# A selective-scan block on one core: the second sequence's input term scaled on ScalarE, ScalarE's longer stages cut into parts, one more slot for the broadcast rows

## The chip, the cores and the metric

The kernel runs on one core of one Trainium2 chip. The metric is the device time of one execution in microseconds; lower is better. Engines are named as the profile names them: PE is TensorE (PEld its weight loads), DVE is VectorE, ACT is ScalarE, POOL is GpSimd, SP is SyncE, which here only issues DMAs; ACTq is the DMA queue that ACT issues into.

## The reference

Two sequences of 1024 tokens with 512 channels (all float32) go through a selective scan and a feed-forward layer, each followed by a residual and a layer norm. Cut to what matters here:

```python
xn = x * rsqrt(mean(x*x) + 1e-6) * norm_w
xn = xn * sigmoid((xn @ select_proj_w.T + select_proj_b) * select_gate)
delta, B, C = split(xn @ x_proj_w.T)
delta = softplus(delta @ dt_proj_w.T + dt_proj_b)
def step(h, dt, b, c, xt):
    h = exp(dt[:, :, None] * A) * h + (dt * xt)[:, :, None] * b[:, None, :]
    return h, einsum('bdn,bn->bd', h, c)
x = layernorm(x + (y + x * D_param) @ out_proj_w.T)
x = layernorm(x + ffn(x))
```

The state h has 2 x 512 x 128 numbers, and each of the 1024 steps needs the state of the step before.

## The kernel before, in words

**The scan.** The 128 state entries lie on the partitions, the 512 channels on the free axis. Per step DVE issues four instructions of 128x512: two products `m = a * h` into PSUM (line 526, one for each sequence) and two of line 536, `h = u * B + m`, a scalar_tensor_tensor that reads m from PSUM, the row u from SBUF and B as a scalar per partition, and writes h to SBUF. Nothing else is on DVE during the scan.

**What feeds a step.** The factor a comes from ACT: line 745 (`exponents`) takes an exponential of a PSUM tile of 2048 columns, one every second step, into a ring of four blocks of four steps; PE makes the tile (line 928) from `dexp`, which POOL makes (line 481). The row u = dt * x is the same on all partitions: SP issues one DMA per step (line 392) that broadcasts it from memory into `u_bc`, a ring of five; the DMA for step t waits for h of step t-5. PE takes h to y (line 942, two steps at a time); DVE may run six steps (`H_RING`) ahead of it.

**The rest of the network** is spread over the scan. The tokens are worked in eight chunks of 128 steps. During chunk c the kernel computes the stages before the scan for chunk c+1 (`stages_before`: RMS norm `sq`, `ms`, `root`, gate `sel`, `gate`, projections `xp`, `dtp`, softplus `soft`, `ut`) and the stages behind it for chunk c-1 (`stages_behind`: `yt`, `outp`, layer norm `ln1`, `vt`, the feed-forward `gu`, `act`, `down`, then `back` and layer norm `ln2`). `timetable` gives each stage a slot, two slots per step, and each engine walks through the slots in program order; a stage's second number in these lists is the gap in slots to the next. The products of these stages share one PSUM bank, so PE's next stage waits until ACT has emptied the last one. Within a step, ACT's loop runs the exponential first and then the stages of the slot. Everything that ACT does stands in one queue, in that order.

**The end.** The last chunk's two halves are worked as two units: the first inside chunk 7, the second behind the scan. For the second, 16 of the 24 weight tiles of 512 KB go into the ring of a as its blocks come free; ACT issues those DMAs (line 682) between its other work.

Of the kernel before, what the change touches and what calls it, by code (L numbers as in the profile page):

```python
# [6 lines left out]
P = 128  # L7
# [52 lines left out]
def stages_before():  # L60

    yield from [("x_in", 0, 6), ("sq", 0, 4), ("ms", 0, 4), ("root", 0, 4)]
    for j in range(2):
        yield "xn", j, 0
    for j in range(2):
        yield from [("sel", 2 * j, 3), ("sel", 2 * j + 1, 4), ("gate", j, 1)]
    yield "mask", 0, 1
    yield "mask", 1, 3
    for j in range(2):
        yield "xs", j, 0  # L70
    for m in range(3):
        yield from [("xp", m, 4), ("xpc", m, 1)]
    for j in range(2):
        yield from [("dtp", j, 3), ("pre", j, 1), ("soft", j, 7), ("c1", j, 0), ("c2", j, 0), ("c3", j, 0), ("c4", j, 0)]
    for b in range(BATCH):
        yield from [("ut", b, 3), ("utc", b, 1)]
# [12 lines left out]
def stages_behind(x):  # L89

    both, ws, wide = x < LAST, halves(x), int(x < LAST - 1)
    ahead = W_RING if both else (TILES_14 if x == LAST else HB)
# [5 lines left out]
    for w in ws:  # L98
        yield from [("yt", w, 2 + wide), ("ymc", w, 2)]
        if x == UNITS - 1:  # L100
            for j in range(TILES_IN_A - TILES_IN_A // A_RING, HB):
                yield "tile", j, 0
        yield from [("outp", 2 * w, 3), ("outp", 2 * w + 1, 3 + wide), ("ln1", w, 2 * w if both else 4)]
# [10 lines left out]
    for m in range(KB):  # L114
        for q in range(4):
            yield "down", 4 * m + q, (2 + q % 2 * wide if both else 1)
            if q % 2 and HB + ahead + 2 * m + q // 2 < TILES:
                yield "tile", HB + ahead + 2 * m + q // 2, 0
        yield "dnc", m, 1
    for w in ws:  # L120
        yield from [("back", w, 3 + wide), ("ln2", w, 1 + wide)]


def timetable(c):
# [3 lines left out]

    plan = {}
    threads = []  # L130
    if c < LAST:
        threads.append([0, c + 1, list(stages_before())])
    if c == LAST:
        threads.append([2 * SLOTS * GP + 4, LAST, list(stages_behind(LAST))])
    if c > 0:
        x = c - 1 if c < CHUNKS else LAST + 1
        threads.append([0, x, list(stages_behind(x))])
    emptied, taken = 0, {}
    while threads:
        thread = min(threads, key=lambda t: t[0])  # L140
        slot, x, stages = thread
# [6 lines left out]
        if first:  # L148
# [5 lines left out]
            emptied = place + 1  # L154
        if stage in PIECES:
# [17 lines left out]
def build(nc, xT, x_rows, vecs, d_row, sel_wT, xproj_wT, dt_wT, out_wT, A_log, gu_w, down_w, out_rows):  # L173
# [5 lines left out]
    with ctx:  # L179
# [10 lines left out]
        mean_mat = sb("mean_mat", [P, P])  # L190
# [35 lines left out]
        stat = sb("stat", [P, 8])  # L226
# [66 lines left out]
        def window_of(x, w):  # L293
# [24 lines left out]
        s_dexp, s_p, s_exp, s_cz, s_m, s_h, s_y, s_ycp = (  # L318
            sem(s) for s in ("s_dexp", "s_p", "s_exp", "s_cz", "s_m", "s_h", "s_y", "s_ycp"))
# [6 lines left out]
        s_xd, s_ya, s_yt, s_outp, s_ln, s_vt, s_gu, s_th, s_sg, s_gm, s_gated, s_down, s_back = (  # L326
            sem(s) for s in ("s_xd", "s_ya", "s_yt", "s_outp", "s_ln", "s_vt", "s_gu", "s_th", "s_sg", "s_gm",
# [40 lines left out]


        def sync(e):  # L370
# [15 lines left out]
            for t in range(SEQ):  # L386
# [116 lines left out]
        def vector(e):  # L503
            e.memset(mean_mat[:, :], 1.0 / D).then_inc(s_const, 1)
# [14 lines left out]
            for t in range(SEQ):  # L519
# [24 lines left out]
        def scalar(e):  # L544
# [3 lines left out]
            def before(x, stage, j):  # L548
# [7 lines left out]
                elif stage == "sq":  # L556
# [4 lines left out]
                    e.activation(T[:, :, :], U[:, :, :], ACT.Square).then_inc(s_sq, 1)  # L561
                    e.wait_ge(s_sq, x + 1)
# [44 lines left out]
                elif stage == "soft":  # L607
                    n = 5 * (2 * x + j)
                    log_table()
                    e.wait_ge(s_work, emptied("dtp", x, j))  # L610
                    if 2 * x + j:
                        e.wait_ge(s_c2, 2 * x + j)
                    if x and j == 0:
                        e.wait_ge(d_us, 16 * BATCH * x)
                    e.activation(t_exp, pre[:, :, :], ACT.Abs).then_inc(s_soft, 1)
                    e.wait_ge(s_soft, n + 1)
                    e.activation(pre[:, :, :], pre[:, :, :], ACT.Relu).then_inc(s_relu, 1)
                    e.activation(t_exp, t_exp, ACT.Exp, scale=-1.0).then_inc(s_soft, 1)
                    e.wait_ge(s_soft, n + 2)
                    if j == 0:  # L620
                        e.wait_ge(s_xs, 2 * (x + 1))
                    e.activation(T[:, both, :], t_exp, ACT.Ln, bias=one[:, :]).then_inc(s_soft, 1)
                    e.activation(t_one, t_exp, ACT.Identity, bias=one[:, :]).then_inc(s_soft, 1)
                    e.wait_ge(s_soft, n + 4)
                    e.activation(t_one, t_one, ACT.Identity, bias=minus_one[:, :]).then_inc(s_soft, 1)
# [8 lines left out]
            def layer_norm(src, turn, x, w, n):  # L634

                rows = v(x, w)
                e.activation(rows, src, ACT.Identity, accum_out=stat[:, 0:1]).then_inc(s_work, 1)
                e.wait_ge(s_work, turn)
                e.activation(stat[:, 1:2], stat[:, 0:1], ACT.Copy, scale=-1.0 / D).then_inc(s_ln, 1)
                e.wait_ge(s_ln, 6 * n + 1)  # L640
                e.activation(rows, rows, ACT.Identity, bias=stat[:, 1:2]).then_inc(s_ln, 1)
                e.wait_ge(s_ln, 6 * n + 2)
                e.activation(squares(x), rows, ACT.Square, accum_out=stat[:, 2:3]).then_inc(s_ln, 1)
                log_table()
                e.wait_ge(s_ln, 6 * n + 3)
# [6 lines left out]
            def place_free(x, j, ahead):

                gone = j - ahead
                if gone < HB:
                    e.wait_ge(s_gu, HB * x + gone + 1)
                else:
                    e.wait_ge(s_down, 4 * KB * x + 2 * (gone - HB) + 2)

            def behind(x, stage, j):  # L660
                if stage == "tile":
                    if x < LAST:
                        if j >= W_RING:
                            place_free(x, j, W_RING)
                        elif x:
                            place_free(x - 1, TILES + j, W_RING)
                    elif x == LAST:
                        if j == 0:
                            e.wait_ge(s_xp, 3 * CHUNKS)
                        elif j == 1:  # L670
                            e.wait_ge(s_dexp, 2 * PER_CHUNK * LAST)
                            e.wait_ge(s_u, 2 * LAST)
# [346 lines left out]
```

## Time and profile before

| what | value |
|---|---|
| median of 3 runs | 2753.72 us (2746.35 to 2754.31) |
| the profiled execution: its time, its span | 2745.6 us, 2743.8 us |
| DVE busy | 2605.7 us, 95% |
| PE busy | 2346.4 us, 86% |
| ACT busy | 1540.3 us, 56% |
| POOL busy | 844.9 us, 31% |
| mean granted TensorE clock | 0.955 of full speed |

Shares are averages over the span. An engine's idle time is put down to whoever released it last; "issue" is time for which the profile shows no wait. The rows below are from the profiled execution.

### The profile page before, as it was taken

What the parts mean: (1) busy time and instruction counts of PE and PEld (TensorE: products, weight loads), DVE (VectorE), ACT (ScalarE), POOL (GpSimd) and SP (SyncE); (2) the same over time, 40 slices, a digit from 0 to 9 for tenths busy, and PEclk for the clock granted to TensorE, in tenths of its full rate; (3) what the DMA queues carried; (4) which work ended last, traced back from release to release, by engine and by line L of the source; (5) the groups of instructions that cost most, each with busy time, mean ns of one, the idle gap of its engine ahead of it and who ended that gap; (6) DMA issues with size and microseconds to landing.
All of it is one profiled execution on the core that took longest, in us unless ns stands there. A gap on an engine that the chain in (4) does not pass through costs nothing.

```text
span 2743.8 us, 46936 instructions
## 1 busy us (share of the span) xinstructions
PE 2346.4 (86%) x17024; PEld 1290.3 (47%) x17024; DVE 2605.7 (95%) x4134; ACT 1540.3 (56%) x1957; POOL 844.9 (31%) x765
## 2 busy tenths in 40 slices
PE   4776677999779987899879997799978998899877
PEld 3322224555345543455435553455534554465557
DVE  2999999999999999999999999999999999999970
ACT  5554345664666555664556646566466655654733
POOL 2222222342324423343233433244232442243310
PEclk8999999999899999999989999999999999999988
DMA  3556665777657776677767786577766787688782
GB/s 131 207 208 217 218 231 208 262 278 272 240 201 280 278 259 234 222 279 280 264 211 242 277 286 241 205 271 270 269 241 217 276 279 261 237 295 300 258 324 91
DMA packets 192465, 673.65 MB, mean 246 GB/s; under 512 B 20976, under 2 KB 26096, under 8 KB 192240
## 3 DMA queue, kind: packets, MB, share of 16 engines
q1 hardware_dynamic: 152304, 544.81, 56.2%
q10 hardware_dynamic: 39936, 125.85, 13.5%
q8 instruction: 140, 2.29, 0.3%
q14 instruction: 85, 0.70, 0.1%
HBM read 662.18 MB, written 8.39 MB: 244 GB/s over the span
## 4 chain that ended last, share of the span: by engine, by line
DVE 51%; PE 22%; issue 17%; ACT 8%; DMA 1%; POOL 0%; ACTq 0%; POOLq 0%; DVEq 0%
DVE h L536 32%; DVE banks L526 19%; PE banks L796 7%; PE banks L928 5%; PE banks L942 3%; ACT a L745 3%; PE banks L905 2%; PE banks L875 1%; ACT L546 1%; PE banks L871 1%; DMA w_xp<-in_down_w 1%; PE banks L880 1%; DMA U<-in_xT 1%; ACT dt L582 0%; PE banks L872 0%
## 5 line engine op out<-in xcount | busy, mean ns | idle before, releaser
L745 ACT ACTIVATE a<-banks 128x2048 f32<-128x2048 f32 x512 | 961.3, 1878 | 861.6 <-PE banks L928 707.3
L536 DVE SCALAR_TENSOR_TENSOR h<-u_bc,BCt,banks 128x512 f32<-128x512 f32 x2048 | 1426.9, 735 | 15.4 <-PE banks L942 15.2
L526 DVE TENSOR_TENSOR banks<-a,h 128x512 f32<-128x512 f32 x2048 | 1326.4, 690 | 9.4 <-ACT a L745 9.4
L481 POOL TENSOR_TENSOR dexp<-spread,dt 128x512 f32<-128x512 f32 x512 | 539.7, 1054 | 1423.2 <-DVE banks L526 1353.2
L942 PE MATMUL banks<-h,cz 128*32 128x512 f32 x4096 | 714.7, 625 | 112.8 <-DVE h L536 111.8
L928 PE MATMUL banks<-dexp,A 32*128 32x256 f32 x8192 | 615.3, 416 | 125.0 <-ACT a L745 124.1
L928 PEld LDWEIGHTS banks<-dexp,A 32*128 32x128 f32 x8192 | 385.4, 192 | 460.4 <-ACT a L745 307.6
L796 PE MATMUL banks<-vT,w_ring 128*128 128x256 f32 x1792 | 446.7, 392 | 7.6 <-ACT up L714 6.9
L796 PEld LDWEIGHTS banks<-vT,w_ring 128*128 128x128 f32 x1792 | 322.0, 189 | 174.6 <-issue 118.2
L942 PEld LDWEIGHTS banks<-h,cz 128*32 128x32 f32 x4096 | 110.0, 109 | 402.9 <-issue 395.1
L905 PE MATMUL banks<-gated,w_ring 128*128 128x256 f32 x896 | 223.5, 392 | 8.9 <-ACT vT L719 6.7
L905 PEld LDWEIGHTS banks<-gated,w_ring 128*128 128x128 f32 x896 | 160.9, 189 | 92.7 <-issue 61.1
L712 ACT ACTIVATE sg<-banks 128x256 f32<-128x256 f32 (+1 forms) x144 | 52.0, 361 | 173.3 <-PE banks L796 171.8
L796 PE MATMUL banks<-U,w_sel 128*128 128x256 f32 x256 | 76.6, 453 | 43.3 <-ACT gated L689 20.8
L450 POOL TENSOR_TENSOR gated<-gated,sg 128x512 f32<-128x512 f32 x56 | 71.6, 1278 | 82.4 <-DVE banks L526 82.4
L453 POOL TENSOR_TENSOR gated<-gated,up 128x512 f32<-128x512 f32 x56 | 71.5, 1277 | 82.4 <-DVE banks L526 82.4
L796 PEld LDWEIGHTS banks<-U,w_sel 128*128 128x128 f32 x256 | 54.5, 223 | 75.2 <-ACT gated L689 26.2
L546 ACT ACT_TABLE_LOAD x57 | 73.1, 1283 | 1.7 <-PEq L1011 0.7
L716 ACT ACTIVATE sg<-sg,half 128x256 f32<-128x256 f32 (+1 forms) x144 | 71.3, 495 | 0.0
L796 PE MATMUL banks<-U,w_xp 128*128 128x256 f32 x192 | 47.3, 391 | 11.0 <-ACT BCt L598 7.9
L875 PE MATMUL banks<-w_out,gated 128*128 128x512 f32 x60 | 36.6, 742 | 23.3 <-ACT dt L582 11.5
L714 ACT ACTIVATE up<-banks 128x256 f32<-128x256 f32 (+1 forms) x144 | 52.8, 366 | 0.0
(134 smaller groups left out, 1147.7 us busy)
## 6 DMA issues: line engine op xcount, KB each, us to landing
u_bc<-u_scratch SPq DMA_DIRECT2D x1024, 512.0 KB, 4.6
w_ring<-in_gu_w ACTq DMA_DIRECT2D x112, 512.0 KB, 5.3
w_ring<-in_down_w ACTq DMA_DIRECT2D x56, 512.0 KB, 5.4
a<-in_gu_w ACTq DMA_DIRECT2D x16, 512.0 KB, 6.8
U<-in_xT ACTq DMA_DIRECT2D x8, 512.0 KB, 6.4
u_scratch<-t_both ACTq DMA_DIRECT2D x16, 256.0 KB, 4.4
a<-in_down_w ACTq DMA_DIRECT2D x8, 512.0 KB, 4.2
x_tok<-in_x_rows SPq DMA_DIRECT2D x15, 256.0 KB, 6.1
```

What stands on the lines that cost most here:

```text
L450: e.tensor_tensor(pair, pair, sg[:, ring, 0:columns_of(x)], ALU.mult).then_inc(s_gm, 1)
L453: e.tensor_tensor(pair, pair, up[:, ring, 0:columns_of(x)], ALU.mult).then_inc(s_gated, 1)
L481: e.tensor_tensor(dexp[:, q % E_RING, :, :, :], spread[:, :].unsqueeze(1).unsqueeze(1).to_broadcast(shape), by_step[:, :, first:first + BS ...
L526: e.tensor_tensor(m_ps[:, b, :], a[:, blk % A_RING, b, s, :], h[:, (t - 1) % H_RING, b * D:(b + 1) * D], ALU.mult).then_inc(s_m, 1)
L536: e.scalar_tensor_tensor(h[:, t % H_RING, part], u_bc[:, t % U_RING, part], BCt[c % 2][:, 0, b * TB + tl:b * TB + tl + 1], m_ps[:, b, :], ...
L546: e.preload_act_table_set("natural_log_exp_and_others")
L716: e.activation(gate, gate, ACT.Identity, bias=half[:, :], scale=0.5).then_inc(s_sg, 1)
L745: e.activation(dst.rearrange("p b t (x j) -> p x (b t) j", j=GP), src.rearrange("p g (i r j) -> p (g i) r j", i=PAIR, j=GP), ACT.Exp, scal ...
L796: last = e.matmul(dst, w, x, start=i == 0, stop=i == len(pairs) - 1)
L905: last = e.matmul(dst, tile[:, sub * (HB // 4) + i, :], hidden(x, hb), start=hb == 0, stop=hb == HB - 1)
L928: last = e.matmul(dst[:, g, i * COLS:(i + 1) * COLS], A[rows, q % 2 * PAIR + i, :], lays, start=True, stop=True)
L942: last = e.matmul(y_ps[group * GP:(group + 1) * GP, :], cz[:, first:first + GP], h[:, t % H_RING, b * D:(b + 1) * D], start=i == 0, stop=i ...
```

## The change

DVE's second line-536 instruction becomes a plain sum. A new ACT instruction per step, `scaled(t)`, multiplies the second sequence's half of `u_bc` by B in place, and the sum adds it to m:

```diff
 U_RING = 5 -> 6,  E_RING = 4 -> 3,  CZ_RING = 3 -> 2
+Z_AHEAD = 2
 def vector(e):
-    for b in range(BATCH):
-        e.scalar_tensor_tensor(h[:, t % H_RING, part], u_bc[:, t % U_RING, part], BCt[...], m_ps[:, b, :], ALU.mult, ALU.add)
+    e.wait_ge(s_m, BATCH * t + 1)
+    e.scalar_tensor_tensor(h[:, t % H_RING, 0:D], u_bc[:, t % U_RING, 0:D], BCt[...], m_ps[:, 0, :], ALU.mult, ALU.add)
+    e.wait_ge(s_m, BATCH * t + 2)
+    e.wait_ge(s_z, t + 1)
+    e.tensor_tensor(h[:, t % H_RING, D:], m_ps[:, 1, :], u_bc[:, t % U_RING, D:], ALU.add).then_inc(s_h, 1)
 def scalar(e):
+    def scaled(t):
+        e.wait_ge(d_u[t % U_RING], 16 * (t // U_RING + 1))
+        row = u_bc[:, t % U_RING, D:]
+        e.activation(row, row, ACT.Copy, scale=BCt[c % 2][:, 0, TB + tl:TB + tl + 1]).then_inc(s_z, 1)
     for i in range(SLOTS):
         if SLOTS * t + i in EXP_AT:
             exponents(EXP_AT[SLOTS * t + i], p_ps)
+        if i == 0 and t + Z_AHEAD < SEQ:
+            scaled(t + Z_AHEAD)
 def stages_before():
-    ("sq", 0, 4) ... ("pre", j, 1), ("soft", j, 7)
+    ("sq", 0, 2), ("sq", 1, 2) ... ("pre", j, 2), ("soft", 3 * j, 2), ("soft", 3 * j + 1, 3), ("soft", 3 * j + 2, 2)
 def stages_behind(x):
-    ("ln1", w, 2 * w if both else 4) ... ("ln2", w, 1 + wide)
+    ("ln1", w, 2), ("ln1b", w, 2 * w if both else 2) ... ("ln2", w, 1 + wide), ("ln2b", w, 0)
 def timetable(c):
-        thread = min(threads, key=lambda t: t[0])
+        thread = min(threads, key=lambda t: (t[0], t[3]))
 def sync(e):
+    for j in range(TILES):
+        if j < TILES_IN_A:
+            e.wait_ge(s_m, BATCH * BS * (BLOCKS - A_RING + j // (TILES_IN_A // A_RING) + 1))
+        else:
+            place_free(e, LAST + 1, j, TILES_IN_A)
+        weights(e, LAST + 1, j)
```

The squares of `sq` and its scaling are two stages; softplus is three (Abs and Relu; table, Exp and Ln; two Identity); a layer norm is two (`ln1`: mean, centring, squares; `ln1b`: table, root, scaling), with sums kept in two sets of columns. The matrix of 1/512 for `ms` becomes one column that is broadcast, which gives room for the sixth slot of `u_bc`; `cz` is filled one block ahead instead of two. The last unit's weight tiles are issued by SP, behind all rows of u, and no longer by ACT.

How the order moves, at three places. First ACT in chunk 1, around the second layer norm of the unit behind (its line 637 to 650, in the change 664 to 680; 745 is the exponential, in the change 765; 775 is `scaled`; 701 and 719 copy the transposed norm). Before:

```order
L582 ACTIVATE dt<-banks,half_gate_bias,half_gate 128x256 x2
L587 ACTIVATE dt<-dt,half 128x512 x2
L745 ACTIVATE a<-banks 128x8x8x32 x2
L637 ACTIVATE v,stat<-banks 128x512
L639 ACTIVATE stat<-stat 128x1
L641 ACTIVATE v<-v,stat 128x512
L643 ACTIVATE gated,stat<-v 128x512
L546 ACT_TABLE_LOAD
L646 ACTIVATE stat<-stat,eps_ln 128x1
L648 ACTIVATE stat<-stat 128x1
L650 ACTIVATE v<-v,stat 128x512
L745 ACTIVATE a<-banks 128x8x8x32
```

Now:

```order
L765 ACTIVATE a<-banks 128x8x8x32
L775 ACTIVATE u_bc<-u_bc,BCt 128x512
L664 ACTIVATE v,stat<-banks 128x512
L666 ACTIVATE stat<-stat 128x1
L668 ACTIVATE v<-v,stat 128x512
L670 ACTIVATE gated,stat<-v 128x512
L775 ACTIVATE u_bc<-u_bc,BCt 128x512
L565 ACT_TABLE_LOAD
L676 ACTIVATE stat<-stat,eps_ln 128x1
L678 ACTIVATE stat<-stat 128x1
L680 ACTIVATE v<-v,stat 128x512
L765 ACTIVATE a<-banks 128x8x8x32
```

The norm now has one `scaled` between its two parts, every exponential is followed by one or two, and the norm stands ahead of the second gate instead of behind it.

Second, ACT in chunk 1 at the softplus of the first half (lines 615 to 625; in the change 637 to 651; 712 and 730 are the feed-forward's tanh). Before:

```order
L604 ACTIVATE pre<-banks,vec 128x256 x2
L546 ACT_TABLE_LOAD
L615 ACTIVATE t_both<-pre 128x512
L617 ACTIVATE pre<-pre 128x512
L618 ACTIVATE t_both<-t_both 128x512
L622 ACTIVATE dt<-t_both,one 128x512
L623 ACTIVATE t_both<-t_both,one 128x512
L625 ACTIVATE t_both<-t_both,minus_one 128x512
L745 ACTIVATE a<-banks 128x8x8x32
L712 ACT_TABLE_LOAD
```

Now:

```order
L637 ACTIVATE t_both<-pre 128x512
L639 ACTIVATE pre<-pre 128x512
L775 ACTIVATE u_bc<-u_bc,BCt 128x512
L565 ACT_TABLE_LOAD
L642 ACTIVATE t_both<-t_both 128x512
L646 ACTIVATE dt<-t_both,one 128x512
L765 ACTIVATE a<-banks 128x8x8x32
L775 ACTIVATE u_bc<-u_bc,BCt 128x512
L730 ACT_TABLE_LOAD
L730 ACTIVATE sg<-banks 128x256
```

The six instructions are spread, with the feed-forward's table load and tanh now inside them. Third, SP's queue at the end, where u_bc is line 404 (before 392) and the last unit's tiles were on ACT:

```order
L396 DMA U<-in_x_rows 128x512
L404 DMA u_bc<-u_scratch 128x1024 x96
L396 DMA x_tok<-in_x_rows 128x512
L404 DMA u_bc<-u_scratch 128x1024 x15
L379 DMA a<-in_gu_w 128x1024 x16
L379 DMA a<-in_down_w 128x1024 x8
```

SP's queue ended with the fourth of these rows; the last two are new there, behind every row of u.

## Rows read from the trace of the kernel before

**Rows 1.** The page's busy times and its chain that ended last, by engine.
```profile
PE 2346.4 (86%) x17024; PEld 1290.3 (47%) x17024; DVE 2605.7 (95%) x4134; ACT 1540.3 (56%) x1957; POOL 844.9 (31%) x765
DVE 51%; PE 22%; issue 17%; ACT 8%; DMA 1%; POOL 0%; ACTq 0%; POOLq 0%; DVEq 0%
```
**Rows 2.** Groups by line: shapes, count | busy us, mean ns | idle before, releasers.
```profile
L536 DVE SCALAR_TENSOR_TENSOR h<-u_bc,BCt,banks 128x512 f32<-128x512 f32 x2048 | 1426.9, 735 | 15.4 <-PE banks L942 15.2
L526 DVE TENSOR_TENSOR banks<-a,h 128x512 f32<-128x512 f32 x2048 | 1326.4, 690 | 9.4 <-ACT a L745 9.4
L745 ACT ACTIVATE a<-banks 128x2048 f32<-128x2048 f32 x512 | 961.3, 1878 | 861.6 <-PE banks L928 707.3 <-DVE banks L526 152.8 <-ACT v L650 1.5
```
**Rows 3.** Timeline of DVE at 1400 us: start, us, engine, line, operation.
```profile
1400.65 1.28 DVE L526 TENSOR_TENSOR banks<-a,h 128x512 f32<-128x512 f32 x2
1401.85 1.39 DVE L536 SCALAR_TENSOR_TENSOR h<-u_bc,BCt,banks 128x512 f32<-128x512 f32 x2
1403.17 1.28 DVE L526 TENSOR_TENSOR banks<-a,h 128x512 f32<-128x512 f32 x2
```
**Rows 4.** Timeline of DVE ahead of the scan.
```profile
11.38 1.29 DVE L410 TENSOR_TENSOR U<-U,rstd 128x512 f32<-128x512 f32 x2 [5.05 <-ACT rstd L576]
```
**Rows 5.** Groups of ACT, shapes kept apart.
```profile
L650 ACT ACTIVATE v<-v,stat 128x512 f32<-128x512 f32 x30 | 21.7, 722 | 1.0
L617 ACT ACTIVATE pre<-pre 128x512 f32<-128x512 f32 x16 | 10.1, 631 | 0.5
```
**Rows 6.** Timeline of ACT, chunk 2, around the second layer norm.
```profile
780.47 1.88 ACT L745 ACTIVATE a<-banks 128x2048 f32<-128x2048 f32 x1 [2.96 <-PE banks L928]
782.24 0.59 ACT L637 ACTIVATE v<-banks 128x512 f32<-128x512 f32 x1
784.69 1.28 ACT L546 ACT_TABLE_LOAD   x1
786.54 0.72 ACT L650 ACTIVATE v<-v,stat 128x512 f32<-128x512 f32 x1
787.17 1.86 ACT L745 ACTIVATE a<-banks 128x2048 f32<-128x2048 f32 x1
```
**Rows 7.** Timeline of DVE, chunk 2, the same stretch.
```profile
780.75 1.39 DVE L536 SCALAR_TENSOR_TENSOR h<-u_bc,BCt,banks 128x512 f32<-128x512 f32 x2
795.13 1.41 DVE L536 SCALAR_TENSOR_TENSOR h<-u_bc,BCt,banks 128x512 f32<-128x512 f32 x2 [1.70 <-PE banks L942]
```
**Rows 8.** Windows of chunk 2: us, busy by engine, granted clock, DMA share, GB/s.
```profile
742.00:792.00 50.00, 36.82 (x270) 19.90 (x270) 50.00 (x80) 29.94 (x38) 13.06 (x12) 0.89 0.60 209
792.00:868.00 76.00, 71.70 (x545) 41.57 (x545) 74.31 (x119) 49.05 (x63) 25.99 (x23) 0.98 0.71 246
868.00:944.00 76.00, 72.79 (x523) 41.55 (x525) 76.00 (x122) 47.72 (x67) 32.37 (x28) 1.00 0.78 276
```
**Rows 9.** Waits inside 742 to 792 us: total, times, longest.
```profile
ACT a L745 <- PE banks L928: 19.7, 7, 5.9
```
**Rows 10.** Timeline at the scan's start.
```profile
61.50 2.14 DVE L526 TENSOR_TENSOR banks<-a,h 128x512 f32<-128x512 f32 x2
72.61 2.14 DVE L526 TENSOR_TENSOR banks<-a,h 128x512 f32<-128x512 f32 x2
```
**Rows 11.** The chain that ended last and DVE's timeline near the scan's end.
```profile
2633.05 16.74 DMA w_xp<-in_down_w
...
2653.87 1.41 DVE L536 SCALAR_TENSOR_TENSOR h<-u_bc,BCt,banks 128x512 f32<-128x512 f32 x2 [3.27 <-PE banks L942]
```
**Rows 12.** DMA issues: count, KB each, us to landing.
```profile
u_bc<-u_scratch SPq DMA_DIRECT2D x1024, 512.0 KB, 4.6
```
**Rows 13.** Timeline of DVE and PE around the scan's end.
```profile
2661.62 1.40 DVE L536 SCALAR_TENSOR_TENSOR h<-u_bc,BCt,banks 128x512 f32<-128x512 f32 x2
...
2688.76 30.75 PE L796 MATMUL banks<-vT,a 128*128 128x128 f32 x256 [0.73 <-ACT vT L701]
```

More of the change, by code:

```diff
@@ L91, in stages_behind @@
     both, ws, wide = x < LAST, halves(x), int(x < LAST - 1)
-    ahead = W_RING if both else (TILES_14 if x == LAST else HB)
+    ahead = W_RING if both else TILES_14
     if x <= LAST:
@@ L99, in stages_behind @@
         yield from [("yt", w, 2 + wide), ("ymc", w, 2)]
[L100 to L103, printed above, removed]
+        yield from [("outp", 2 * w, 3), ("outp", 2 * w + 1, 3 + wide), ("ln1", w, 2), ("ln1b", w, 2 * w if both else 2)]
     for w in ws:
@@ L120, in stages_behind @@
     for w in ws:
-        yield from [("back", w, 3 + wide), ("ln2", w, 1 + wide)]
+        yield from [("back", w, 3 + wide), ("ln2", w, 1 + wide), ("ln2b", w, 0)]
 def timetable(c):
@@ L555, in before @@
                                 ).then_inc(d_x, 16)
[L556 removed]
+                elif stage == "sq" and j == 0:
                     e.wait_ge(d_x, 16 * (x + 1))
@@ L618, in before @@
[L618 to L625, printed above, removed]
+                    half_d, part = j // 3, j % 3
@@ L652, in place_free @@
[L652 to L658, printed above, removed]
+                e.activation(st[:, 1:2], st[:, 0:1], ACT.Copy, scale=-1.0 / D).then_inc(s_ln_a, 1)
+                e.wait_ge(s_ln_a, 3 * n + 1)
+                e.activation(rows, rows, ACT.Identity, bias=st[:, 1:2]).then_inc(s_ln_a, 1)
+                e.wait_ge(s_ln_a, 3 * n + 2)
@@ L766, in scalar @@
             columns(0)
-            columns(1)
             for q in range(2):
                 exponents(q, (p_ps, banks[:, G:, :])[q])
+            for t in range(Z_AHEAD):
+                scaled(t)
             for t in range(SEQ):
@@ L773, in scalar @@
                     window(t // WIN - 1)
-                if t % CS == 5 and t // CS + 2 < SEQ // CS:
-                    columns(t // CS + 2)
-                if t % BS == 1 and t > SEQ - BS * A_RING + BS:
-                    gone = t // BS - (BLOCKS - A_RING) - 1
-                    for j in range(TILES_IN_A // A_RING):
-                        behind(LAST + 1, "tile", gone * (TILES_IN_A // A_RING) + j)
+                if t % CS == 4 and t // CS + 1 < SEQ // CS:
+                    columns(t // CS + 1)
                 for i in range(SLOTS):
@@ L811, in before @@
                     e.wait_ge(s_sq, x + 1)
-                    product(dst[:, 0:TC], [(mean_mat[:, :], T[:, k, :]) for k in range(KB)]).then_inc(s_ms, 1)
+                    product(dst[:, 0:TC], [(mean_col[:, :].to_broadcast([P, P]), T[:, k, :]) for k in range(KB)]).then_inc(s_ms, 1)
                 elif stage == "sel":
```

158 lines of the change are left out of this document (89 added, 69 removed).

## The prediction

> **What bounds the kernel now.** I read the busy times first: DVE is busy 95% of the span, PE 86%, ACT 56%, and the chain that ended last lies on DVE for half of its length [rows 1]. The groups by line show why: DVE's time is 4096 instructions of two lines, and both together idled for only 25 us [rows 2]. In the timeline a pair of line 526 starts at 1400.65, the pair of line 536 at 1401.85, the next pair of line 526 at 1403.17 [rows 3]: 0.60 us a product, 0.66 us a scaled sum (their listed lengths overlap), 2.52 us a step. 1024 steps are 2580 of the 2743.8 us. So DVE's issue rate is the bound, and only what shortens a step or makes DVE wait counts. ACT does 1540 us of work, but 862 us of its idle time stands in front of line 745, and 707 of those were waits for PE [rows 2]: it is not free to do other work then, since its queue runs in order.
>
> **The change part by part.**
>
> *DVE's fourth instruction.* A sum of m (PSUM) and u (SBUF) takes the place of the same sum with a multiplication by a per-partition scalar. The trace has no sum that reads PSUM without such a scalar. The nearest rows bound it. Line 536 reads and writes the very same tiles: 0.66 us, a gain of 0. Line 526 reads SBUF and writes PSUM at 0.60 us, and line 410, all in SBUF, has two instructions in 1.29 us of which the second lasts 0.69, so 0.60 to start the second [rows 2 to 4]; that end is a gain of 0.06 x 1024 = 61 us. I take 0, since line 536 shares its operands and differs by the scalar alone. What speaks for the other end is ACT: there a scalar read per partition lengthens an instruction of 128x512 from 631 to 722 ns [rows 5], so the 0.06 us could be the scalar's price. A loss on DVE I exclude: the new instruction reads one operand less.
>
> The Trainium skill (Perfetto Trace Analysis, Optimizing Scalar/DVE Operations) puts DVE's access overhead at about 60 ns for SBUF and 125 ns for PSUM. By it the difference of 0.06 us is the price of reading PSUM, it stays, and this part is worth nothing; the rows agree in size but cannot tell PSUM from the scalar.
>
> *ACT's new instruction.* `scaled` has the form of line 650, a copy of 128x512 with a scale per partition: 0.72 us [rows 5]. 1024 of them are 737 us, which brings ACT to 2277 us, 83% of the span. On average that fits. What matters is where it stands: behind everything ahead of it in ACT's queue, and DVE waits for it every step, with the exponential's waits for PE in front of it.
>
> I placed it in the trace. Counting pairs of line 536 from the scan's start, step 285 is the pair that starts at 780.75, so its second half starts at 781.41 [rows 7]. In the old order the instruction for step 285 would have stood behind the layer norm that ends at 786.54 + 0.72 = 787.26 [rows 6], and ended at 787.98: 6.6 us late. DVE is delayed in this stretch anyway by 1.70 us, when y on PE is six steps behind [rows 7], so 4.9 us are new. The split of the norm takes the part from the table load on, 784.69 to 787.26, behind the `scaled` between its parts: 2.6 us less, 2.3 left. The exponential ahead of the norm had itself waited 2.96 us for PE, which the split doesn't mend.
>
> Then the added work. From 742 to 792 us ACT was busy 29.9 of 50 us [rows 8], and 19.7 us of the rest were waits of line 745 for PE [rows 9]. These 50 us are 20 steps, so 14.3 us of `scaled` come in. If the waits absorb them, nothing is lost; if none is absorbed, 29.9 + 14.3 + 19.7 exceeds 50 by 13.9 us. PE in turn waits for ACT in this stretch, since one bank is handed to and fro, so a delay of one comes back through the other; that speaks against the lower end. I take half, 7 us. The next two stretches have 49.1 and 47.7 us of ACT in 76 [rows 8]; with 21.7 us added they reach 70.8 and 69.4 and still fit, so I charge them nothing; what covers them are the 5 to 7 us that remain, and softplus beside the first tanh (second pair of order rows) is the place where that cover is thinnest.
>
> Per chunk 2.3 + 7 = 9.3 us, in the six chunks 1 to 6 that have both kinds of stages: 56 us. Bounds: 0, and 4.9 + 13.9 = 18.8 a chunk, 113 us.
>
> *The start.* DVE already waits for exponentials there: products that take 2.14 instead of 1.28 us [rows 10]. Ten steps of filling the ring get 0.72 us of ACT each: 7 us, bounds 0 and 8.
>
> *Ring of six, the rows' DMAs.* The landing takes 4.6 us [rows 12], the sixth slot lets it start one step (2.52 us) earlier, and `scaled` wants the row two steps earlier than DVE did. 6 steps less 2 are 10 us, so the landing is covered; if contention took it to 10, ACT's queue would stand.
>
> *The end.* A tile for unit 14 landed 16.74 us after its issue, behind four tiles for the ring of a on the same queue; PE waited, and DVE 3.27 us for PE [rows 11]. With SP issuing those four behind the rows of u this wait should go: -3 us. Against it, chunk 7 has PE on the chain throughout, and `scaled` ties DVE closer to PE there: 0 to +14. I put the two together at 0. SP's first tiles go out behind the last rows of u, some five steps (13 us) before the scan's end; the first is used at 2688.76, 26 us behind it [rows 13], so I cost that at nothing.
>
> *The rest* (smaller `dexp` and `cz` rings, the broadcast column, seven more table loads at most) is nothing as long as POOL (31%) and ACT's idle time hide it; a smaller `cz` ring gives ACT one more wait for y.
>
> Sum: 0 + 56 + 7 + 0 = +63 on the profiled 2745.6: 2809 us. The profiled execution lies 8 us under the median of the three runs, at their lower edge; I leave the forecast on its level.
>
> **Rivals.**
>
> 1. *The scalar was the price, ACT still late.* DVE gains 61 us, but not in the 20 of 128 steps a chunk where ACT and PE set the pace (8 us over six chunks): 2809 - 61 + 8 = 2756. For it: rows 5. Chance 0.18.
> 2. *The scalar was the price, and the waits absorb the work*: 2745.6 - 61 + 6 x 2.3 + 7 = 2705. This is the side that is faster; it decides as soon as the plain sum starts its successor after 0.60 us and DVE's wait for `scaled` stays below 9 us a chunk. For it: ACT has 20 us idle in the tight stretch. Against it: 6.6 us of lateness in the old order. Chance 0.17. The Trainium skill, same section, says that moving work to ScalarE may make sense when DVE is saturated; by that it would be this case, and the trace bears out only that DVE is saturated.
> 3. *Nothing gained, little lost* (the change doesn't do what it says, DVE's step stays at 2.52 us and ACT is on time): 2745.6 + 14 + 7 = 2767. Chance 0.13.
> 4. *The loop between ACT and PE takes all of it*: 113 + 7 = +120, 2866. For it: TensorE's granted clock was already 0.89 in the tight stretch, between its levels of 1.2 and 2.4 GHz [rows 8], after waits of PE for ACT; longer waits could bring more of it. Chance 0.12.
>
> The forecast itself has 0.40.
>
> **How the numbers follow.** A measurement of this kernel can tell about 0.3% (8 us) from no change. Slower: the forecast, rivals 3 and 4 and a third of rival 1, less 0.03 of rival 3 that ends within 0.3%: 0.68. Same: 0.10. Faster: rival 2 and 0.05 of rival 1: 0.22. The range runs from rival 2 to rival 4, 2705 to 2866; the forecast's own, with none or all of the 14 us a chunk instead of half, from 2767 to 2851.
>
> **What would show it.** Right: the instruction after the new sum starts 0.66 us behind it; a step at rest is 2.52 us; DVE gets a new wait for ACT's `u_bc`, some 9 us in each of chunks 1 to 6, most of it between steps 12 and 34 of a chunk; ACT's busy time is near 2280 us; the wait of 16.7 us for a tile near the end is gone. Wrong on DVE: steps of 2.46 us. Wrong on ACT: the wait for `u_bc` is under 2 us a chunk. Wrong on place: the wait sits at the softplus (steps 55 to 90), or in front of `scaled` for the rows' DMA. A time below 2737 would refute the forecast as a whole.

## The result and the profile after

The changed kernel takes 2907.5 us (median of 4 runs, 2907.1 to 2908.6), the kernel before in the same comparison 2751.7 us (2746.4 to 2754.3): a ratio of 1.057 (95% interval 1.055 to 1.059), 156 us slower. The forecast was 63 us slower. The profiled span is 2905.7 us, 161.9 more than before.

The page's busy times and its chain, by engine and by line, now read (compare [rows 1]):

```profile
PE 2365.6 (81%) x17024; PEld 1317.5 (45%) x17024; DVE 2571.0 (88%) x4134; ACT 2150.2 (74%) x2988; POOL 843.5 (29%) x765
PE 52%; ACT 23%; DVE 12%; issue 10%; DMA 1%; ACTq 1%; DVEq 0%; POOLq 0%; POOL 0%; SPq 0%
PE banks L823 19%; PE banks L955 13%; PE banks L932 8%; PE banks L969 8%; ACT a L765 7%; ACT u_bc L775 6%; DVE banks L545 5%; DVE h L553 4%; DVE h L557 3%; ACT L565 2%; PE banks L902 1%; PE banks L898 1%; ACT v L668 1%; ACT sg L730 1%; ACT L730 1%
```

DVE went from half of the chain to an eighth, and PE has taken its place, although PE does the same 17024 matmuls in nearly the same time. In the changed kernel 545 is the product, 553 the scaled sum, 557 the plain sum, 765 the exponential, 775 `scaled`, 955 PE's tile for the exponential, 969 y, 823 the products of the feed-forward's first layer (`gu`) among others, and 730 to 734 the stage `act`, which reads the bank that `gu` filled and so empties it.

The groups by line (compare [rows 2]):

```profile
L545 DVE TENSOR_TENSOR banks<-a,h 128x512 f32<-128x512 f32 x2048 | 1350.2, 707 | 9.5 <-ACT a L765 9.5
L765 ACT ACTIVATE a<-banks 128x2048 f32<-128x2048 f32 x512 | 960.9, 1877 | 590.6 <-PE banks L955 520.4 <-DVE banks L545 63.5 <-ACT v L680 3.4
L553 DVE SCALAR_TENSOR_TENSOR h<-u_bc,BCt,banks 128x512 f32<-128x512 f32 x1024 | 764.5, 747 | 0.0
L557 DVE TENSOR_TENSOR h<-banks,u_bc 128x512 f32<-128x512 f32 x1024 | 707.5, 691 | 208.4 <-ACT u_bc L775 208.1
L775 ACT ACTIVATE u_bc<-u_bc,BCt 128x512 f32<-128x512 f32 x1024 | 702.7, 719 | 19.4 <-DMA u_bc<-u_scratch 7.3 <-PE banks L932 6.2 <-ACT v L680 3.0
```

Line 557 has a wait of 208 us for `scaled`, which was not there before. Where nothing waits, DVE's timeline reads (compare [rows 3]):

```profile
301.50 0.74 DVE L557 TENSOR_TENSOR h<-banks,u_bc 128x512 f32<-128x512 f32 x1
302.10 1.35 DVE L545 TENSOR_TENSOR banks<-a,h 128x512 f32<-128x512 f32 x2
303.30 0.80 DVE L553 SCALAR_TENSOR_TENSOR h<-u_bc,BCt,banks 128x512 f32<-128x512 f32 x1
303.95 0.74 DVE L557 TENSOR_TENSOR h<-banks,u_bc 128x512 f32<-128x512 f32 x1
304.56 1.35 DVE L545 TENSOR_TENSOR banks<-a,h 128x512 f32<-128x512 f32 x2
```

The product starts 0.60 us after the plain sum, where 0.66 had passed before, and from product to product a step is 2.46 us instead of 2.52. That is also the median over all steps, so DVE's step did become shorter, by 63 us in all, and the kernel lost some 225 us elsewhere.

**Where it lost them.** For each kernel I took the time from the first product of a step to the first product of the next, less the median step of that kernel, and summed what lies over it. Steps are counted within a chunk; the middle columns are means of chunks 1 to 6, us per chunk:

```
kernel      step   chunk 0 | steps 0-11  12-35  36-55  56-95  96-127 | chunk 7
before      2.521     2.2  |        0.0    1.1    0.0    0.0     0.0 |    14.2
changed     2.459    10.1  |        0.2    7.2    0.2   22.8     3.0 |    33.9
```

6 x (33.4 - 1.1) = 194 us in chunks 1 to 6, 20 in chunk 7, 8 in chunk 0, 5 ahead of the scan (its start varies from 57 to 63 us over the kernels of this study, whatever they change), less 63 for the shorter steps and 1 behind the scan: 163, within 1 us the 162 of the spans. 137 us of it, the larger part, lie in steps 56 to 95 of a chunk, the feed-forward's `gu` and `act`, which the prediction charged nothing.

**What happens there.** ACT's timeline in the changed kernel, chunk 2, a stretch of a few us, and below it PE's:

```profile
919.91 1.88 ACT L765 ACTIVATE a<-banks 128x2048 f32<-128x2048 f32 x1 [2.06 <-PE banks L955]
921.68 0.71 ACT L775 ACTIVATE u_bc<-u_bc,BCt 128x512 f32<-128x512 f32 x1
922.29 0.37 ACT L730 ACTIVATE sg<-banks 128x256 f32<-128x256 f32 x1
922.56 0.38 ACT L731 ACTIVATE gated<-banks 128x256 f32<-128x256 f32 x1
922.82 0.39 ACT L732 ACTIVATE up<-banks 128x256 f32<-128x256 f32 x1
```

```profile
916.77 2.00 PE L823 MATMUL banks<-vT,w_ring 128*128 128x256 f32 x8
918.69 1.15 PE L955 MATMUL banks<-dexp,A 32*128 32x256 f32 x16
919.77 1.07 PE L969 MATMUL banks<-h,cz 128*32 128x512 f32 x8
923.26 2.00 PE L823 MATMUL banks<-vT,w_ring 128*128 128x256 f32 x8 [2.43 <-ACT up L732]
```

PE finished `gu` at 918.8. `act` could have emptied the bank at once, since ACT was idle for 2.06 us; but an exponential stands ahead of it in ACT's queue, and the exponential needs PE's next tile (919.84). So ACT waits for the tile, runs the exponential (1.88), then `scaled` (0.71), then `act`, and PE, which has meanwhile only its y to do, idles for 2.43 us. The same work before, in chunk 2, PE's timeline and then ACT's:

```profile
868.48 1.15 PE L928 MATMUL banks<-dexp,A 32*128 32x256 f32 x16
869.55 1.99 PE L796 MATMUL banks<-vT,w_ring 128*128 128x256 f32 x8
871.48 1.06 PE L942 MATMUL banks<-h,cz 128*32 128x512 f32 x8
872.47 1.15 PE L928 MATMUL banks<-dexp,A 32*128 32x256 f32 x16
```

```profile
878.50 0.38 ACT L712 ACTIVATE sg<-banks 128x256 f32<-128x256 f32 x1 [2.94 <-PE banks L796]
878.78 0.38 ACT L713 ACTIVATE gated<-banks 128x256 f32<-128x256 f32 x1
879.04 0.39 ACT L714 ACTIVATE up<-banks 128x256 f32<-128x256 f32 x1
879.71 1.89 ACT L745 ACTIVATE a<-banks 128x2048 f32<-128x2048 f32 x1
```

Here either PE's tile comes ahead of `gu` (868.48), so that the exponential runs beside `gu`, or `act` comes ahead of the exponential (878.50, 879.71), and PE has no gap. The new gaps in the lists of stages and the new rule that picks a thread in `timetable` moved `act` by one slot, half a step, against the exponentials, which stand in every fourth slot: of the 16 `act` of a chunk 14 now have an even slot, and 7 of these the very slot of an exponential, behind it. Before, all 16 stood in odd slots.

The windows of steps 60 to 91 of chunk 2, before and changed (columns as in [rows 8]), and then the changed kernel's waits there (total, times, longest):

```profile
859.48:940.15 80.67, 77.69 (x558) 44.45 (x552) 80.67 (x129) 51.95 (x73) 34.71 (x31) 1.00 0.78 277
```

```profile
891.75:989.75 98.00, 79.23 (x530) 46.72 (x531) 80.53 (x129) 69.23 (x104) 34.61 (x31) 0.92 0.66 229
```

```profile
ACT a L765 <- PE banks L955: 29.5, 11, 3.8
PEld banks L823 <- ACT up L732: 19.6, 9, 4.6
DVE h L557 <- ACT u_bc L775: 17.4, 9, 3.8
PE banks L823 <- ACT up L732: 13.9, 5, 4.2
```

PE was busy for 77.7 of 80.7 us before: it had 3 us to spare in 32 steps. ACT had 29 to spare, and still has 29. The limit is not the amount of ACT's work but its place: PE waits for ACT and ACT for PE in turn. TensorE's granted clock is 0.92 in this stretch, in which PE waits, and was 1.00 before, when it hardly did: part of the stretch runs at the lower of its two levels. PE's busy time rises by 1.5 us only, so most of the 17 us are idle time.

### The profile page after: what moved, and what is told of

Same layout as the page of the kernel before. It is cut to its first block, busy times and chain, and to the rows that moved or that the text cites. A ratio compares the mean times of both kernels' runs of the same rounds, so it can differ in the third digit from the quotient of the medians.

```text
span 2905.7 us, 48999 instructions
## 1 busy us (share of the span) xinstructions
PE 2365.6 (81%) x17024; PEld 1317.5 (45%) x17024; DVE 2571.0 (88%) x4134; ACT 2150.2 (74%) x2988; POOL 843.5 (29%) x765
## 4 chain that ended last, share of the span: by engine, by line
PE 52%; ACT 23%; DVE 12%; issue 10%; DMA 1%; ACTq 1%; DVEq 0%; POOLq 0%; POOL 0%; SPq 0%
PE banks L823 19%; PE banks L955 13%; PE banks L932 8%; PE banks L969 8%; ACT a L765 7%; ACT u_bc L775 6%; DVE banks L545 5%; DVE h L553 4%; DVE h L557 3%; ACT L565 2%; PE banks L902 1%; PE banks L898 1%; ACT v L668 1%; ACT sg L730 1%; ACT L730 1%
## 5 line engine op out<-in xcount | busy, mean ns | idle before, releaser
L545 DVE TENSOR_TENSOR banks<-a,h 128x512 f32<-128x512 f32 x2048 | 1350.2, 707 | 9.5 <-ACT a L765 9.5
L557 DVE TENSOR_TENSOR h<-banks,u_bc 128x512 f32<-128x512 f32 x1024 | 707.5, 691 | 208.4 <-ACT u_bc L775 208.1
L553 DVE SCALAR_TENSOR_TENSOR h<-u_bc,BCt,banks 128x512 f32<-128x512 f32 x1024 | 764.5, 747 | 0.0
L969 PE MATMUL banks<-h,cz 128*32 128x512 f32 x4096 | 676.4, 629 | 94.7 <-DVE h L557 91.4
L955 PE MATMUL banks<-dexp,A 32*128 32x256 f32 x8192 | 623.9, 421 | 158.5 <-ACT a L765 156.8
L775 ACT ACTIVATE u_bc<-u_bc,BCt 128x512 f32<-128x512 f32 x1024 | 702.7, 719 | 19.4 <-DMA u_bc<-u_scratch 7.3
L955 PEld LDWEIGHTS banks<-dexp,A 32*128 32x128 f32 x8192 | 391.8, 196 | 509.4 <-ACT a L765 370.1
L823 PE MATMUL banks<-vT,w_ring 128*128 128x256 f32 x1792 | 493.4, 423 | 135.8 <-ACT up L732 110.7
L823 PEld LDWEIGHTS banks<-vT,w_ring 128*128 128x128 f32 x1792 | 351.5, 206 | 320.7 <-ACT up L732 155.6
L969 PEld LDWEIGHTS banks<-h,cz 128*32 128x32 f32 x4096 | 103.4, 110 | 354.4 <-issue 336.1
```

Of the source, the lines that this page charges most:

```text
L545: e.tensor_tensor(m_ps[:, b, :], a[:, blk % A_RING, b, s, :], h[:, (t - 1) % H_RING, b * D:(b + 1) * D], ALU.mult).then_inc(s_m, 1)
L553: e.scalar_tensor_tensor(h[:, t % H_RING, 0:D], u_bc[:, t % U_RING, 0:D], BCt[c % 2][:, 0, tl:tl + 1], m_ps[:, 0, :], ALU.mult, ALU.add).t ...
L557: e.tensor_tensor(h[:, t % H_RING, D:], m_ps[:, 1, :], u_bc[:, t % U_RING, D:], ALU.add).then_inc(s_h, 1)
L775: e.activation(row, row, ACT.Copy, scale=BCt[c % 2][:, 0, TB + tl:TB + tl + 1]).then_inc(s_z, 1)
L823: last = e.matmul(dst, w, x, start=i == 0, stop=i == len(pairs) - 1)
L955: last = e.matmul(dst[:, g, i * COLS:(i + 1) * COLS], A[rows, q % 2 * PAIR + i, :], lays, start=True, stop=True)
```

## The experiments

Theory 1: the delay comes through PE, which hands over a bank and waits for ACT behind an exponential and a `scaled`. Theory 2: DVE itself waits for a `scaled` that is late, as line 557's 208 us say at first sight. Theory 3: the rest of the change (smaller rings, stages in parts, their new places) costs it.

**Load, sum and wait apart.** Four kernels, all from the changed one. In the two with a load, ACT's instruction reads A and writes one of two spare tiles (`u_bc` has five slots again, for room). In rest_sum and load_sum the factor B of the second sequence is left out:

```diff
 rest_only, rest_sum:
-            for t in range(Z_AHEAD): scaled(t)
-                    if i == 0 and t + Z_AHEAD < SEQ: scaled(t + Z_AHEAD)
 load_only, load_sum:
-                row = u_bc[:, t % U_RING, D:]
-                e.activation(row, row, ACT.Copy, scale=BCt[...])
+                e.activation(spare[:, t % 2, :], A[...], ACT.Copy, scale=BCt[...])
 all four:
-                e.wait_ge(s_z, t + 1)
 rest_only, load_only: the second sum is a scalar_tensor_tensor with B again
```

> The changed kernel without scaled: DVE scales by B again for both sequences, everything else of the change stays (stages in parts, smaller rings, sixth slot, last tiles on SP). Theory 1 (scaled stands on ACT between the exponential and the emptying of the one bank, and PE has no slack there): the rest is harmless, 2740 to 2760 us. Theory 2 (DVE waits for a late scaled, PE only follows): the same, 2740 to 2760. Theory 3 (the smaller rings and the new order of stages are what costs): 2800 or more.

> The changed kernel without scaled and without DVE's wait for it, but with the plain sum on DVE: the factor B of the second sequence is left out. A step at rest is 2.46 us as in the changed kernel. If DVE alone bounds the scan, 61 us less than rest_only, about 2685 us. Theory 1 says less than that, since PE was busy 72 of 74 us in the stretch of the feed-forward, 2.45 us a step: a gain of 40 to 60 us, 2690 to 2710. Theory 3: over 2750.

> As rest_only, but ACT runs the 1024 added instructions at their places, into spare memory that nobody reads: DVE never waits for them. Theory 1: the delay comes through PE, so nearly all of it stays, 2860 to 2910 us. Theory 2: without DVE's wait it is gone, 2750 to 2780. Theory 3: as rest_only.

> As load_only with the plain sum on DVE (factor B of the second sequence left out): ACT's load is there and DVE never waits for it. It differs from the changed kernel by the wait alone. Theory 1: within 30 us of the changed kernel's 2907, 2870 to 2910, and within 30 us of load_only, since DVE's shorter step is hidden behind PE where the time is lost. Theory 2: 2690 to 2720.

Measured, medians in us and the ratio to before with its interval (before: 2751.3):

| | B on DVE | plain sum |
|---|---|---|
| no `scaled` | rest_only 2791.9, 1.014 (1.010 to 1.017) | rest_sum 2738.7, 0.995 (0.994 to 0.997) |
| ACT's load, no wait on DVE | load_only 2915.6, 1.059 (1.057 to 1.061) | load_sum 2904.2, 1.056 (1.054 to 1.058) |
| with the wait | | changed 2907.5, 1.057 (1.055 to 1.059) |

Theory 2 falls: without DVE's wait the time is the same within the intervals. (load_sum also has the ring of five, and its load waits for no row of u; in the changed kernel ACT waited 7.3 us in all for rows.) The wait of 208 us is where the delay shows, not where it arises; in load_sum, DVE's groups show it as waits for y on PE and as longer products:

```profile
L546 DVE TENSOR_TENSOR banks<-a,h 128x512 f32<-128x512 f32 x2048 | 1457.9, 754 | 8.9 <-ACT a L765 8.9
L554 DVE SCALAR_TENSOR_TENSOR h<-u_bc,BCt,banks 128x512 f32<-128x512 f32 x1024 | 751.7, 734 | 96.7 <-PE banks L971 96.2 <-DMA u_bc<-u_scratch 0.2
```

The load by itself costs 124 us with B on DVE (2915.6 - 2791.9) and 166 with the plain sum. The plain sum gains 53 us where ACT has room and 11 where it hasn't. And rest_only is 41 us slower than before, although it has no `scaled` and ACT is busy only 8 us more (seven table loads): part of theory 3 is right. That is why rest_only and rest_sum missed what was expected of them, 2740 to 2760 and 2690 to 2710. By stretch, us per chunk as in the table above:

```
kernel      step   chunk 0 | steps 0-11  12-35  36-55  56-95  96-127 | chunk 7
rest_only   2.521     3.6  |        0.0    0.1    0.0    7.4     0.0 |    19.0
rest_sum    2.461     4.6  |        0.2    0.2    0.1    7.4     0.2 |    23.7
load_only   2.521     4.5  |        0.0    4.3    0.8   20.9     0.8 |    28.6
load_sum    2.461     5.3  |        0.5    7.8    1.2   23.7     1.0 |    33.1
```

In chunks 1 to 6 the rest costs only at the feed-forward, 7.4 us a chunk; the load adds 13.5 and 16.3 in the same place.

**The places of the stages.** Four more, again from the changed kernel: `act` ahead of the exponential within its slot; `scaled` behind the stages of its slot; the timetable of before with `scaled`; and that timetable without it.

```diff
 act_first:
+                    behind(x, stage, j) for the "act" of this slot
                     exponents(...)
                     scaled(t + Z_AHEAD)
                     all other stages of this slot
 late:
                     exponents(...)
-                    scaled(t + Z_AHEAD)
                     all stages of this slot
+                    scaled(t + Z_AHEAD)
 old_slots, old_slots_rest:
-    ("sq", 0, 2), ("sq", 1, 2)
+    ("sq", 0, 0), ("sq", 1, 4)
-    ("pre", j, 2), ("soft", 3 * j, 2), ("soft", 3 * j + 1, 3), ("soft", 3 * j + 2, 2)
+    ("pre", j, 1), ("soft", 3 * j, 0), ("soft", 3 * j + 1, 0), ("soft", 3 * j + 2, 7)
     (ln1 with ln1b and ln2 with ln2b likewise in one slot)
-        thread = min(threads, key=lambda t: (t[0], t[3]))
+        thread = min(threads, key=lambda t: t[0])
```

> The changed kernel; only the order inside a slot on ACT differs: the stage that empties the bank of the feed-forward (act) goes ahead of the exponential and of scaled of the same slot, where it stood behind both. Theory 1 (PE hands the bank over and then waits for an exponential and a scaled that it does not need): steps 56 to 96 of a chunk lose 2 to 5 us instead of 23, steps 12 to 36 still 7, so 2907 less 7 x 19, about 2775 us. Rival (ACT is simply too full there, 0.72 us more in each step, wherever it stands): 2860 or more.

> The changed kernel with scaled behind all stages of its slot instead of ahead of them; the exponential stays in front. Theory 1: PE's wait loses the 0.71 us of scaled but keeps the 1.75 of the exponential, so steps 56 to 96 go back to what they lose without scaled (5 to 11 us instead of 23), about 2810 us; DVE then waits more in steps 12 to 36, where the layer norm stands ahead of scaled, up to 5 us a chunk: 2810 to 2840. Rival (ACT too full): 2880 or more.

> The changed kernel with the timetable of the kernel before: the parts of softplus, squares and layer norm stand in one slot again, act in odd slots, half a step away from the exponentials; scaled, the plain sum, the smaller rings and the last tiles on SP stay. Theory 1: steps 56 to 96 lose 3 to 8 us instead of 23, since act behind an exponential still has one scaled ahead of it; steps 12 to 36 lose 9 to 12, since the norm is whole again: 2770 to 2800 us. Rival (ACT too full): 2860 or more. Rival (the split is what lets scaled through, so without it ACT is later): over 2907.

> As old_slots without scaled and with B on DVE for both sequences: what is left of the change are the smaller rings, the sixth slot, the broadcast column and the last tiles on SP. If the 40 us that rest_only loses come from the new places of the stages, this is the kernel before within 10 us, 2740 to 2760. If they come from the smaller rings, it stays at 2780 to 2795.

Measured (before: 2749.6): act_first 2788.7 us, ratio 1.015 (1.013 to 1.017); late 2842.6, 1.034 (1.032 to 1.037); old_slots 2826.1, 1.028 (1.026 to 1.030); old_slots_rest 2744.2, 0.997 (0.996 to 0.998).

```
kernel          step   chunk 0 | steps 0-11  12-35  36-55  56-95  96-127 | chunk 7
act_first       2.461    12.2  |        0.2    8.7    0.2    1.7     3.7 |    28.6
late            2.461     9.7  |        0.2    8.3    0.2   12.4     2.3 |    28.7
old_slots       2.461    10.4  |        0.2   13.4    2.5    1.2     3.7 |    26.4
old_slots_rest  2.521     2.9  |        0.0    1.3    0.0    0.0     0.0 |    13.0
```

One swap inside a slot gives back 119 of the 156 us: act_first loses 1.7 us where the changed kernel loses 22.8. Its windows of the same 32 steps, and those of old_slots:

```profile
873.14:953.11 79.97, 73.98 (x547) 43.33 (x540) 79.59 (x130) 69.73 (x107) 34.66 (x31) 1.00 0.80 280
```

```profile
886.33:965.82 79.49, 75.20 (x551) 43.34 (x549) 79.49 (x130) 69.93 (x105) 34.70 (x31) 1.00 0.80 278
```

Both carry all of `scaled` (ACT 70 us of 80), and both run the stretch in less time than the kernel before (80.67 us), with the clock at 1.00. So the load fits there; theory 1 holds, and "ACT too full" falls. The 41 us of rest_only are the places too: with the old ones they are gone. late takes `scaled` alone from ahead of `act`: 10 of the 22.8 us go, and 12.4 stay with the exponential still in front.

I had expected 2775 for act_first and 2770 to 2800 for old_slots. In act_first I had counted chunk 7 like the other six, 19 us to gain, and it gained 5 (33.9 to 28.6). In old_slots I had named only steps 12 to 35 and 56 to 95; chunk 7 keeps 26.4 us, and steps 36 to 55 and 96 to 127 lose 2.5 and 3.7 us a chunk, 37 in all, for which no run shows the reason. In its steps 12 to 35, with the norm whole again and norm and gate at their old places, 13.4 us are lost instead of 7.2. So the parts and the new places are worth 6 us a chunk there; no run tells the two apart.

**Prices on DVE.** In the kernel before, the second sequence's sum takes one of four forms, by t % 4:

```diff
+  form 0: scalar_tensor_tensor(dst, row, BCt[...], m, mult, add)
+  form 1: scalar_tensor_tensor(dst, row, 0.5, m, mult, add)
+  form 2: tensor_tensor(dst, m, row, add)
+  form 3: tensor_tensor(dst, row, row, add)
```

> The kernel before, DVE alone: the fourth instruction takes a different form in each of four steps: scale by a scalar per partition and add (as before), the same with a constant 0.5 in place of the scalar, a plain sum of m and u, a plain sum of u with itself that reads no PSUM (the last three leave out B, the last also m). If the scalar read per partition is the price: 0.66 us to the next instruction in the first form, 0.60 in the other three. If the two operations of one instruction are: 0.66, 0.66, 0.60, 0.60. If reading PSUM is: 0.66, 0.66, 0.66, 0.60; the changed kernel's 0.60 already speaks against this.

From the start of each to the start of the next instruction the medians are 658, 598, 601 and 603 ns (256 of each). A stretch of the timeline, where 539 is form 0, 541 form 1, 543 form 2 and 526 the product behind each:

```profile
1405.64 0.73 DVE L539 SCALAR_TENSOR_TENSOR h<-u_bc,BCt,banks 128x512 f32<-128x512 f32 x1
1406.30 0.67 DVE L541 SCALAR_TENSOR_TENSOR h<-u_bc,banks 128x512 f32<-128x512 f32 x1
1406.90 1.35 DVE L526 TENSOR_TENSOR banks<-a,h 128x512 f32<-128x512 f32 x2
1408.16 0.73 DVE L539 SCALAR_TENSOR_TENSOR h<-u_bc,BCt,banks 128x512 f32<-128x512 f32 x1
1408.82 0.68 DVE L543 TENSOR_TENSOR h<-banks,u_bc 128x512 f32<-128x512 f32 x1
1409.42 1.28 DVE L526 TENSOR_TENSOR banks<-a,h 128x512 f32<-128x512 f32 x2
```

The scalar read per partition is the price, 60 ns; a second operation in the instruction costs nothing, and neither does reading m from PSUM.

**A version faster than both.** Old places, and `scaled` with the plain sum only in a part of the steps. select_late moves `scaled` to the end of the step's second slot, select_wide does so for more steps:

```diff
+def by_act(t):
+    c, tl = t // TB, t % TB
+    return tl >= 16 if c == 0 else tl < 36 if c == CHUNKS - 1 else tl < 10 or 56 <= tl < 96
-                    if i == 0 and t + Z_AHEAD < SEQ:
+                    if i == 0 and t + Z_AHEAD in Z_INDEX:
```

> As old_slots, but scaled and the plain sum only in 448 of 1024 steps: from step 16 on in chunk 0, steps 0 to 9 and 56 to 95 in chunks 1 to 6, steps 0 to 35 in chunk 7; the others scale by B on DVE. Theory 1 (ACT's added work costs only where PE waits behind it): 448 x 0.06 = 27 us gained on old_slots_rest, some 9 lost at the feed-forward, 2726 us, under both kernels. Rival (every scaled costs PE something, wherever it stands): 2745 or more.

> As select, with scaled at the end of a step's second slot, behind its stages, and so behind act also where act follows the exponential: theory 1 says that the loss at the feed-forward goes, 2717 to 2724 us. Rival: as select.

> As select_late with 756 steps: in chunks 1 to 6 all but steps 10 to 39, in chunk 7 up to step 55. 308 more steps gain 18 us; if the stretches 40 to 56 and 96 to 128 lose what they lost in old_slots, 6 us a chunk, 36 us in all, it ends at 2735 to 2745; if those losses too come from scaled standing ahead of a stage, 2705 to 2715.

Measured (before: 2753.6): select 2733.8 us, ratio 0.994 (0.992 to 0.995); select_late 2743.1, 0.997 (0.996 to 0.998); select_wide 2767.8, 1.006 (1.004 to 1.007). select is faster than both kernels, by 0.6% and 6%. Against old_slots_rest it gains 10 us (spans: 13), not the 18 expected (448 sums at 0.06 us are 27, less 9 at the feed-forward); 8 of the 27 are met again in the last section. The other two go against what I expected: behind the stages of the second slot `scaled` is no better placed, and steps 36 to 55 and 96 to 127 lose more (3.1 and 1.1 us a chunk over a step of 2.521) than their plain sums gain. At that place it stands directly ahead of the next step's exponential, which may be why; no run tells that apart.

## Why the prediction was wrong

*DVE's fourth instruction* was priced at 0.66 us, the end of the bounds at which nothing is gained. It takes 0.60; a step became shorter by 0.06 us, the other bound, and rest_sum against rest_only shows 53 us of it in the time. The choice went by the row that shares all operands but one; that one operand, the scalar, was the price, and the hint from ACT [rows 5] was right. The Trainium skill (Perfetto Trace Analysis, Optimizing Scalar/DVE Operations) names an overhead of about 60 ns for SBUF and 125 ns for PSUM; here 601 ns with m read from PSUM and 603 ns without it show no such difference, and the measurement decides.

*ACT's new instruction* is the step that failed, in one sentence: "The next two stretches ... still fit, so I charge them nothing". The working summed ACT's amounts (70.8 and 69.4 of 76 us), and that sum even erred on the safe side: `scaled` was put at 0.72 us, its listed length, but its successor starts 0.61 us after it (921.68 and 922.29 above), and ACT is busy for 2150.2 us in all where 2277 were forecast. In act_first and old_slots the load does fit, with 69.7 and 69.9 us in 80 and 79.5. But the working took the order of the kernel before for granted. The new timetable put `act` behind the exponential, which costs 7.4 us a chunk by itself (rest_only; with `act` in front, act_first loses 1.7 even with `scaled`), and `scaled` between the two, which brings it to 22.8: 137 us in chunks 1 to 6, charged at 0. The same windows [rows 8] had the warning: PE busy 71.7 and 72.8 of 76 us. I read them for ACT alone.

*The tight stretch* came near the forecast in size: steps 12 to 35 lose 7.2 us a chunk, 6.1 more than before, where the forecast was 9.3. That is in part luck: load_sum loses 7.8 there with no wait of DVE for `scaled`, so the 2.3 us for a late `scaled` are not shown, and the 7 were half of a bound. Another 3.0 are lost in steps 96 to 127, nearly all of it in the last four, of which the forecast had nothing.

*The start*: +7 forecast, 8 measured in chunk 0. The size was right, the reason is not borne out: ACT's load alone adds less than 1 us there (rest_only 3.6, load_only 4.5; rest_sum 4.6, load_sum 5.3), and the changed kernel, in which DVE waits for `scaled`, loses 10.1. *The last chunk*: 0 forecast (bounds -3 and +11), 20 more lost within chunk 7: 5 with the places (14.2 to 19.0, rest_only), 5 with the plain sum (23.7, rest_sum), 9 with the load (33.1, load_sum), 1 with the wait. The text had charged the load alone. In chunk 7, 16 of the 32 `act` stand in even slots and 8 in an exponential's, before the change as after it, so there the new order explains little. In the changed kernel one step there is 7.7 us too long, in a stretch whose chain holds a weight tile that ACT issued and that landed 10.92 us later; why it took so long isn't settled. *The end*: the tile of 16.74 us [rows 11] is gone from the chain, as forecast; a shorter one is there now:

```profile
2812.55 7.26 DMA t_both<-in_down_w
```

With the old places the rest of the change gains 5.5 us (0.997). Sign and size fit the -3 of that step, the place doesn't: the traces show the gain behind the scan, where DVE waits 1.40 us for ACT's last y instead of 6.12. *The ring of six*: rows' landings held `scaled` for 7.3 us in all (line 775's row in the groups), so "covered" was right.

So the direction was right and the account wrong: +56 in chunks 1 to 6 was +194, and 0 for DVE was -63. The time lies above all four rivals. Of the rivals, the first and second had the scalar's price, and the fourth had the loop between ACT and PE, but only in the tight stretch. Two of the signs named came true against the forecast: steps of 2.46 us, and a wait that sits in steps 55 to 90 (22 us a chunk in steps 56 to 95, against 7 in steps 12 to 35, where some 9 were forecast).

## What to carry to other kernels

When engines hand one buffer to and fro, look at what stands in the queue between "full" and "empty", not at how busy the engines are: here a `scaled` of 0.7 us stood ahead of 12 `act` in steps 56 to 95, and with it behind them (late) 10 us a chunk were saved, 0.9 us each, since PE had no slack. A change to a table of gaps is a change to every later stage's phase; list where each stage that empties a shared bank falls against the periodic work, before and after. And a large wait on the engine that ends the chain can be a symptom: take the wait away and keep the load, and see whether the time moves.

## What the runs showed of the hardware

A scalar read per partition costs a DVE instruction of 128x512 60 ns (658 against 598, start to start); ACT's listed lengths differ by 91 (722 against 631 [rows 5]).

Form 3, a sum with both operands in SBUF, starts its successor after 0.60 us in 139 cases and after 1.25 us in 113 (four lie between). In all of the long ones an operation of POOL covers some 0.59 of the instruction, in the short ones hardly ever. DVE's timeline of one, and POOL's:

```profile
1400.02 0.73 DVE L539 SCALAR_TENSOR_TENSOR h<-u_bc,BCt,banks 128x512 f32<-128x512 f32 x1
1400.67 1.32 DVE L545 TENSOR_TENSOR h<-u_bc 128x512 f32<-128x512 f32 x1
1401.92 1.29 DVE L526 TENSOR_TENSOR banks<-a,h 128x512 f32<-128x512 f32 x2
```

```profile
1400.18 1.27 POOL L410 TENSOR_TENSOR U<-U,rstd 128x512 f32<-128x512 f32 x1 [1.41 <-DVE banks L526]
```

In such a case POOL's operation is under way when DVE's instruction starts, and DVE's next one comes 0.47 us after POOL's end (1401.45). The Trainium skill (SBUF — State Buffer, Who interferes with whom) states that a DVE instruction with two SBUF inputs contends with a GpSimd instruction that reads SBUF; the long cases agree.

This took back a part of the gain. The products read a and h, both in SBUF, and POOL's operations are released by them: one of 1.28 us that starts at the end of a step's products was over when the next step's first product came, with sums of 0.66 and 0.66, and is not with 0.66 and 0.60. In the changed kernel DVE's and POOL's timelines show it, a step that is 2.52 us again:

```profile
1012.27 0.68 DVE L557 TENSOR_TENSOR h<-banks,u_bc 128x512 f32<-128x512 f32 x1
1012.88 1.35 DVE L545 TENSOR_TENSOR banks<-a,h 128x512 f32<-128x512 f32 x2
1014.14 0.73 DVE L553 SCALAR_TENSOR_TENSOR h<-u_bc,BCt,banks 128x512 f32<-128x512 f32 x1
```

```profile
1011.78 1.27 POOL L444 TENSOR_TENSOR dt<-dt,pre 128x512 f32<-128x512 f32 x1 [1.41 <-DVE banks L545]
```

The two products take 1.26 us instead of 1.20, since POOL's operation lasts until 1013.05. Of the 1023 products behind a plain sum, 217 are late in this way by 0.06 us, 13 us in all; in select 150 of 448, 8 us; in before, rest_only and old_slots_rest, where the sum takes 0.66, it is 1 to 5 of 1023. In the changed kernel half of the late ones lie in steps 56 to 95, where DVE waits anyway, so they cost less than 13 us there; in select DVE sets the pace in those steps. That a shorter instruction on one engine runs into work of another that it used to cover was in no term of the prediction.
